# GpSimd's gathers in a score stage: begun five groups ahead, or two

## The reference, cut to what matters

```python
xl = (x @ Wl).reshape(n, H, D)
xr = (x @ Wr).reshape(n, H, D)
msg = xl[src] + xr[dst]
act = jnp.where(msg > 0, msg, NEG_SLOPE * msg)
e = jnp.einsum('ehd,hd->eh', act, att)
...
q, k, v = (x @ Wq + bq), (x @ Wk + bk), (x @ Wv + bv)
kv = jnp.einsum('bshd,bshe->bhde', phi(k), v)
```

## Time and profile before

| | us |
|---|---|
| median of the timed runs | 1076.0 |
| lowest and highest | 1075.95, 1079.25 |
| span of the profiled execution | 1150.4 |
| of it: score stage, from 109 to 651 us | 542 |
| PE, DVE, ACT, POOL busy in the stage | 483.7, 375.9, 294.8, 346.7 |

### The profile page before, as it was taken

The page is one execution under the profiler, slowest core; times in us unless marked ns, Lnnn a source line. Parts: engine busy times, 40 slices in busy tenths (PEclk is TensorE's granted clock), DMA queues, the critical chain, the costliest instruction groups (busy, mean ns, idle before and its releaser), DMA issues. The chain is left out here.

```text
span 1150.4 us, 16771 instructions
## 1 busy us (share of the span) xinstructions
PE 1018.2 (89%) x5105; PEld 818.8 (71%) x5105; DVE 840.0 (73%) x1399; ACT 651.4 (57%) x1435; POOL 401.0 (35%) x403
## 2 busy tenths in 40 slices
PE   2797589998999998999899679999999979999995
PEld 1685478988998897989789637888888734444553
DVE  5874267776776776676677969787988467887777
ACT  3263245655555655646456457888999435554442
POOL 0212766666666666667575100010100010000000
PEclk9898788998999999999989889999999989999999
DMA  9263677877777787777776258989999452334314
GB/s 242 39 197 111 217 212 230 235 235 231 230 238 234 229 254 216 230 234 235 228 233 191 95 185 237 323 263 274 281 291 260 142 123 74 93 105 89 84 24 72
DMA packets 109988, 221.88 MB, mean 193 GB/s; under 512 B 25824, under 2 KB 58169, under 8 KB 109793
## 3 DMA queue, kind: packets, MB, share of 16 engines
q1 hardware_dynamic: 89053, 158.63, 41.9%
q0 software_dynamic: 20496, 56.86, 22.0%
q10 hardware_dynamic: 356, 5.32, 1.4%
HBM read 157.79 MB, written 73.53 MB: 201 GB/s over the span
## 5 line engine op out<-in xcount | busy, mean ns | idle before, releaser
L997 POOL DMA_INDIRECT score_gath<-xl_rows,misc x324 | 346.7, 1070 | 171.8 <-issue 99.1
L1037 PE MATMUL score_ps_m<-x_hi,score_w_hi 128*128 128x416 f32 (+1 forms) x576 | 215.0, 373 | 11.6 <-issue 7.9
L1038 PE MATMUL score_ps_m<-x_lo,score_w_hi 128*128 128x416 f32 (+1 forms) x576 | 210.1, 365 | 14.8 <-issue 14.6
L1039 PE MATMUL score_ps_m<-x_hi,score_w_lo 128*128 128x416 f32 (+1 forms) x576 | 209.6, 364 | 8.9 <-issue 8.8
L1169 DVE TENSOR_TENSOR score_zb<-score_gath,score_ps_x 128x1024 f32<-128x1024 f32 x81 | 98.8, 1219 | 158.6 <-remote 129.9
L1689 PE MATMUL ps_all<-agg_gath,agg_hot 128*125 128x256 f32 x648 | 180.3, 419 | 1.8 <-DVE agg_hot L1796 1.8
L1741 ACT ACTIVATE agg_gath<-agg_gath,prob 128x64 f32<-128x64 f32 x648 | 158.9, 338 | 10.2 <-DMA agg_gath<-edge_rows 9.9
L1037 PEld LDWEIGHTS score_ps_m<-x_hi,score_w_hi 128*128 128x128 f32 x576 | 113.2, 196 | 20.9 <-issue 19.2
L1038 PEld LDWEIGHTS score_ps_m<-x_lo,score_w_hi 128*128 128x128 f32 x576 | 113.3, 197 | 18.1 <-issue 16.8
L1039 PEld LDWEIGHTS score_ps_m<-x_hi,score_w_lo 128*128 128x128 f32 x576 | 112.7, 196 | 17.0 <-issue 15.0
L1691 PE MATMUL ps_all<-ext,agg_hot 128*125 128x18 f32 x324 | 117.6, 363 | 0.0
(11 more groups left out here) (331 smaller groups left out, 1622.0 us busy)
## 6 DMA issues: line engine op xcount, KB each, us to landing
edge_rows<-score_gath SPq DMA_DIRECT2D x81, 520.0 KB
agg_gath<-edge_rows SPq DMA_DIRECT2D x81, 520.0 KB, 6.7
local_bc<-local_rows SPq DMA_DIRECT2D x40, 224.0 KB
score_gath<-xl_rows,misc POOLq DMA_INDIRECT x324
xb_rows<-in_x ACTq DMA_DIRECT2D x1, 5000.0 KB, 17.4
phi_c<-phi_rows SPq DMA_DIRECT2D x10, 500.0 KB, 3.9
xb_rows<-in_L_mix_bo POOLq DMA_DIRECT2D x10, 500.0 KB, 7.5
x_bo<-xb_rows SPq DMA_DIRECT2D x10, 500.0 KB
```

What stands on the lines that cost most here:

```text
L997: nc.gpsimd.indirect_dma_start(out=gath[:, g % GS, q, :], out_offset=None, in_=xl_rows, in_offset=bass.IndirectOffsetOnAxis(ap=src_idx[:, ...
L1037: pe.matmul(acc, w_hi[:, i % 2, kk, :], x_hi[:, kk, cols], start=(kk == 0), stop=False)
L1038: pe.matmul(acc, w_hi[:, i % 2, kk, :], x_lo[:, kk, cols], start=False, stop=False)
L1039: mm = pe.matmul(acc, w_lo[:, i % 2, kk, :], x_hi[:, kk, cols], start=False, stop=(kk == KC - 1))
```

## The change

From group 2 on, GpSimd waits before a group's four gathers until VectorE has formed the sum of group g-2. The wait for the sum of group g-5 goes; the other two waits for the slot stay. Nothing else is changed: slots, queues and the other engines' orders are the same.

```diff
     GS = 5
+    AHEAD = 2
...
                 for g in range(NG):
+                    if g >= AHEAD:
+                        pool.wait_ge(s_z, g - AHEAD + 1)
                     if g >= GS:
-                        pool.wait_ge(s_z, g - GS + 1)
                         pool.wait_ge(s_free, g - GS + 1)
                         pool.wait_ge(s_kept[g % GS], 16 * (g // GS))
```

## The result

The changed kernel takes 1202.95 us, median of four runs (1198.28 to 1203.9), beside 1077.62 us for the kernel before (1075.95 to 1080.03, four runs): 1.115 times as long, with an interval of 1.113 to 1.117. That is +125 us, where +47 was forecast and 1156 was the upper end of the range.

What follows compares the result with a forecast made beforehand. The prediction took PE to pace the score stage, with GpSimd running ahead. From the timed 1076 us it added 44 for the weight blocks' chain and 3 for panel weights: 1123 us, stated range 1062 to 1156 (own range 1095 to 1165).

Steps and rivals of the forecast that it cites:

- the chain: SP's weight-block loads wait behind later gathers, delaying maxima, sums and next gathers: +44 us over 22 turns; chance 0.65.
- The signs that were named: Changed profile: maxima idle 3 to 6 us, blocks issued some 5 us ahead, POOL waiting nearly every group, PE idle.
- the weakest step: Attributing the span's 74.4 us above the timed median to PE stalls that timed runs mostly lack; gives 17.03 us per three groups.
- the trace's own scale: Compared with the profiled 19.28 us for three groups, the 19.04 us turn should keep the span within some 20 us of 1150.
- from the end of group 0's last gather to the sum that it released, 1.93 us: Landing time of a group's gathers, read from group 0 and used in the block chain and for `add`: 1.93 us.
- the turn: One round of the block chain, three groups, from POOL's start of group 3n+6 to 3n+9: 19.04 us against 17.03.
- the prediction's long ends (+95): Block landing of 6.7 us and 4.49 us between sums, making the turn 21.3 us: +95 us.
- The masks' sources: cost 0, covered by the block's wait: Mask source loads on SP's even steps, done at 15.0 us before the sum at 16.99: cost 0, else up to 1 us a turn.
- `add` alone would not mind: VectorE's sums waiting for their own gathers: 9.16 us where two groups take 11.4, so cost 0.
- the panel's weights: Third panel's load in SP's step 5, used in ACT's step 3, comes late after the sum of 3: +3 us, once.
- Faster: Rival: stalls are real in timed runs and POOL's run of gathers feeds them; the wait shortens them: 1060 us, chance 0.22.
- No change: Rival: blocks land in 2.6 us instead of 4.6, hiding the turn, or the wait never binds: 1076 to 1079 us, chance 0.13.

Runs made afterwards that it cites:

- e6: Changed kernel with gathers begun four groups ahead instead of two: 1078.59 us, 1.0015 times the kernel before.
- e10: e3 with each group's rows stored a second time to a tensor nobody reads (520 KB more a group): 1132.55 us, 1.051 times the kernel before.
- e1: Changed kernel with the weight blocks' loads moved from SP's step 3n+6 to 3n+3: 1161.15 us, 1.078 times the kernel before.
- e2: Changed kernel with the masks' sources loaded one batch (two groups) earlier in SP's order: 1202.37 us, 1.114 times the kernel before.
- e3: Changed kernel with both moves, blocks at step 3n+3 and masks' sources a batch earlier: 1099.48 us, 1.020 times the kernel before.
- e7: Kernel before, lead of five kept, with the weight blocks' loads moved from SP's step 3n+6 to 3n+9: 1225.06 us, 1.138 times the kernel before.
- e4: Changed kernel with SP's step g storing the rows of group g-2 instead of g: 1099.62 us, 1.018 times the kernel before.
- e8: Kernel before, lead of five kept, with the masks' sources loaded three steps later in SP's order: 1199.48 us, 1.111 times the kernel before.

## Why the prediction was wrong in size, and right in kind

**Right: the chain.** The loads behind `keep` become late, the maxima wait for their blocks, and the sums and PE stand behind them. The signs that were named are there: the maxima idle 6.2 us each (143.6 over 23; 3 to 6 was said), the blocks issued 5.3 us ahead of use (some 5), sums 3n+6 and 3n+7 4.76 us apart (4.3). Three came in another form. POOL waited in 51 groups of 81 instead of 20, where nearly every group was said. PE stood idle before the products, but what it waited for there was the masks. Sums 3n+4 and 3n+6, said to be some 15 us apart, were 17.25.

**Right: the weakest step.** That the trace of before held 74 us of stalls which the timed runs don't have was only argued. It is borne out by 49 later runs of the kernel before: they took 1074.26 to 1082.1 us, and their spans are 1071.7 to 1079.9 us, none near 1150.4. And e6 shows an undisturbed turn of 16.81 us against the 17.03 worked out from it. On the trace's own scale, though, the span was to stay within some 20 us of 1150, and rose by 52.

**Wrong: "from the end of group 0's last gather to the sum that it released, 1.93 us".** This term was mis-sized: 3.24 us measured, 1.31 of the 3.02 us by which the turn was too short, the largest single miss. Group 0 was gathered while the DMA engines were less busy (share 0.48 from 109 to 114 us of before's trace, 0.76 from 193 to 617). The better figure was in the trace of before: over the same 22 turns the store ran 3.23 us after the last gather's end on average (median 2.7), though SP's own lateness is part of that. And e10 shows that this distance depends on what else is under way. The prediction varied the block's landing, which was right, and left this term fixed.

**Wrong in the small terms together:** the block's issue to the maximum took 5.33 us (4.60), the next sum 4.76 (4.30), POOL's start 2.34 (2.05), gathers and issue 5.80 (5.56), together another 1.7 us a turn. The undisturbed turn was 0.22 us shorter than said. 22 times 5.18 makes 114 where 22 times 2.01 made 44. Even the prediction's long ends (+95) come to 1076 + 95 + 3 = 1174 us, above its own range of 1165 and the 1156 that it stated, and short of the 1203 measured.

**Wrong: "The masks' sources: cost 0, covered by the block's wait".** They form a chain that is worth +84 us by itself (e1). A source stands behind the store of g-1, whose gathers start after the sum of g-3, and it serves two groups, so the chain closes over four groups. The prediction's own terms make it 2.05 + 5.18 + 1.93 + 7.9 + 4.3 = 21.4 us, beside 22.7 for four groups: a cover of 1.3 us, and "up to 1 us a turn" was the price if it went. In e1 it took 27.1 us on average (groups 10 to 72), 3.5 us a turn above e6: 3.13 us from the last gather's end to the store instead of 1.93, 7.37 from the store to the mask instead of 5.4, 3.76 from the mask to the sum instead of 2.5, 5.97 to the next sum instead of 4.3. For the total it mattered little, since without it the blocks alone give the same 1202 us (e2). But anyone who had mended only the blocks would have kept two thirds of the loss.

**Wrong: "`add` alone would not mind".** 9.16 us against 11.4 was said for two groups. In e3, the 40 sums of groups 9 to 75 that waited for gathers show on average 2.05 us to POOL's start, 5.27 of gathers and 4.64 from the last gather's end to the sum: 11.96 us, beside 11.2 for two groups at e6's pace. It is again the term of 1.93 us that was too small. The sums waited 85.1 us in all, and the loss was 22 us.

**Wrong: the panel's weights, "+3 us, once".** Sum 9 did come 6 us later than in e6, but by the first block, whose wait the 22 turns do not count. DVE's timeline of the changed kernel:

```profile
178.89 0.69 DVE L1196 TENSOR_REDUCE w_amax<-w_peak 128x32 f32<-128x512 f32 x1 [6.53 <-DMA w_peak<-in_L_ffn_up_w]
179.49 1.21 DVE L1171 TENSOR_TENSOR score_zb<-score_gath,score_ps_x 128x1024 f32<-128x1024 f32 x1
```

The sum before it, of group 8, stands 60.0 us behind the stage's first gather, and 59.7 us in e6. ACT waited 7.53 us for the third panel's weights, 7.40 in e6 and 5.05 in e7, whose lead is five. In e7 sum 8 stands at 57.3 us, so at most 2.7 us can be the weights'.

**The rivals.** Faster: the hole at 124 us did go from the trace, as that rival said, and the time rose all the same. The rival needed the stalls in the timed runs, and the 49 spans above leave no room for them. In e7's trace POOL runs five groups ahead as before (busy 19.1 of the 25 us from 124 us on), and PE ran 91 matmuls there instead of 19. So POOL's run of gathers does not hold PE up, and the rival is refuted. No change: the blocks landed in 4.6 us, not 2.6. The figures behind that estimate, from the Trainium skill, DMA: Bandwidth & Descriptors, section "Anatomy of one DMA", are given there for DMAs that GpSimd issues; the block is loaded from SP's queue.

**The rule about the profile's span.** The section of the Trainium skill that the prediction named (Runtime: NRT & Kernel Launch, "The launch sequence") gives about 6 us between a profile's total and the reported time. That is about two numbers of one execution, and no run here tests it: the profile gives no total besides the span from the first to the last instruction. Where a run has both, its time is 1.7 to 3.0 us above that span (the changed kernel's profiled execution: 1203.9 and 1202.2 us). The reported time of the execution with 1150.4 us is not known; the prediction's 74 us compare it with other executions, so they don't show that the rule fails.

## What to carry to other kernels

SP's queue, which stores in order what POOL gathers, was paced by the gathers' landing, and every load behind a store inherited POOL's lead (e4, e7, e8). So before a lead is cut, list what stands behind each wait and by how much it is early, all of it, as the second chain shows only when the first is gone. Take durations for a closed chain (one whose end releases its next start) from the busy stage, not from the first, quiet group, and give each term of the turn its own bounds, since an error of 3 us comes back 22 times. A chain that is covered by 1 or 2 us in a sum of estimates should be priced by itself.

## What the runs showed that had not been expected

The profiled execution of the kernel before had a span 74 us above the median of the timed runs. From 124 to 149 us its PE matmuls stood 1.3 us apart, at a granted clock of 0.59 (near the lower of the two levels, 1.2 GHz), and between the sums of groups 9 and 75 PE was busy 93% of the time, where e6 shows nearly 100%. In all the other kernels that are shown here, the two with a lead of five and late loads among them, span and median lie within some 6 us of each other, and so do the spans of the kernel before's 49 later runs. Why that one execution ran so was not tried, and stays open.
